# Scores of two heads in two row groups of the TensorE array, in units of two full PSUM banks, maximum unit beside exponential unit

## The reference, cut to what matters

```
qkv = x @ Wqkv + bqkv                      # 16 heads of 16 dimensions
att = softmax(mask(q @ k.T * 16**-0.5))    # causal, 512 x 512 for each head
y   = (att @ v) @ Wout + bout
x1  = layernorm(x + y)
h   = silu(x1 @ w1.T * s1) * (x1 @ w2.T * s2)     # 256 -> 1024
h   = gelu(h @ h1.T * sh1);  h = gelu(h @ h2.T * sh2)   # 1024 -> 1024, twice
out = layernorm(x1 + h @ w3.T * s3)               # 1024 -> 256
```

## Time and profile before

| | |
|---|---|
| median of 2 runs | 2169.16 us (2168.17 to 2170.16) |
| span of the profiled execution | 2166.8 us |
| TensorE, matmuls | 2118.4 us busy (98% of the span) |
| VectorE, ScalarE, GpSimd | 1259.9 (58%), 1316.1 (61%), 492.9 us (23%) |
| chain that ended last | TensorE 89% of it |
| score matmuls in that chain | maxima (line 1116) 7%, exponentials (line 1104) 6% |

### The profile page before, as it was taken

The page is one execution under the profiler, slowest core; times in us unless marked ns, Lnnn a source line. Parts: engine busy times, 40 slices in busy tenths (PEclk is TensorE's granted clock), DMA queues, the critical chain, the costliest instruction groups (busy, mean ns, idle before and its releaser), DMA issues.

```text
span 2166.8 us, 52048 instructions
## 1 busy us (share of the span) xinstructions
PE 2118.4 (98%) x16294; PEld 1878.8 (87%) x16294; DVE 1259.9 (58%) x3928; ACT 1316.1 (61%) x2807; POOL 492.9 (23%) x899
## 2 busy tenths in 40 slices
PE   8789999999999999999999999999999999999998
PEld 4368889989889888899989889988999898988998
DVE  7765555556555565556556565565556556565452
...
PEclk9889999999999999999999999999999999999999
...
GB/s 275 239 120 63 77 71 70 61 81 64 90 65 61 82 74 69 75 69 73 61 81 64 90 64 62 81 76 73 71 76 70 56 82 69 83 64 37 37 6 10
DMA packets 95940, 167.69 MB, mean 77 GB/s; under 512 B 19204, under 2 KB 38404, under 8 KB 95672
## 3 DMA queue, kind: packets, MB, share of 16 engines
...
## 4 chain that ended last, share of the span: by engine, by line
PE 89%; DVE 1%; DMA 0%; issue 0%; SPq 0%; ACT 0%; POOL 0%; POOLq 0%; DVEq 0%
PE ring L1241 44%; PE ring L1226 10%; PE pM L1116 7%; PE pS L1104 6%; PE pO L1164 6%; PE ring L1254 5%; PE ring L1176 4%; PE ring L1206 2%; PE ring L1196 2%; PE ring L1148 1%; PE ring L1215 1%; DMA qk_d<-c 0%; SPq L614 0%; DVE full_g L960 0%; DMA Qs<-nm 0%
## 5 line engine op out<-in xcount | busy, mean ns | idle before, releaser
L921 DVE CUSTOM_DVE_ANT_0 pM<-pM,mask 128x512 f32<-128x512 f32 (+3 forms) x1024 | 498.7, 502 | 366.1 <-PE pM L1116 292.3
L1241 PE MATMUL ring<-Yhi,H 128*128 128x256 f32 x1984 | 501.7, 289 | 0.0
L1241 PE MATMUL ring<-Xhi,H 128*128 128x256 f32 x1984 | 497.9, 288 | 0.0
L1241 PE MATMUL ring<-Ylo,H 128*128 128x256 f32 x1984 | 489.2, 282 | 0.0
L1241 PE MATMUL ring<-Xlo,H 128*128 128x256 f32 x1984 | 486.4, 282 | 0.0
L1241 PEld LDWEIGHTS ring<-Ylo,H 128*128 128x128 f32 x1984 | 377.8, 190 | 7.2 <-issue 3.4
L1241 PEld LDWEIGHTS ring<-Yhi,H 128*128 128x128 f32 x1984 | 377.0, 190 | 7.1 <-issue 3.4
L1241 PEld LDWEIGHTS ring<-Xlo,H 128*128 128x128 f32 x1984 | 379.1, 191 | 0.8
L1241 PEld LDWEIGHTS ring<-Xhi,H 128*128 128x128 f32 x1984 | 378.4, 191 | 1.0 <-issue 0.2
L1116 PE MATMUL pM<-Ks,Qs 128*128 128x512 f32 x992 | 304.2, 340 | 20.6 <-DVE mx L921 9.0
L865 ACT ACTIVATE Yhi<-ring,cols 128x256 fp32r<-128x256 f32 x248 | 117.8, 475 | 266.8 <-PE ring L1241 170.1
...
## 6 DMA issues: line engine op xcount, KB each, us to landing
...
```

Source lines behind the costliest of these rows:

```text
L921: nc.vector.tensor_tensor_reduce(pM[:, h % 2, 0:n], pM[:, h % 2, 0:n], mask[:, T - n:T], 1.0, NEG, ALU.add, ALU.max, mx[:, t, h:h + 1]).th ...
L1241: mm = nc.tensor.matmul(to, w, x_part, start=(k == 0 and m == 0), stop=(k == KB - 1 and m == 1))
```

## The change

- `Qs` and `Qx` lose the dimension that held each head alone: a stack has both heads of a pair in its rows, as `Ks` has. The zeros (two memsets on VectorE, two on GpSimd, semaphores `pads`, `pads_x`) go, and in the head one ScalarE copy takes the place of two.
- A score matmul takes the 50 rows of one head only, at partition 0 or at partition 64: two heads of a pair lie in two row groups of the array, and write to two banks of `pS` or `pM` (bank `s` for head `s`).
- A group has five steps `exp:off:g:e` and five steps `max:off:g:e`. Step e = 0, 1 is 512 columns of pair e; e = 2, 3 is 384 and 128 columns (blocks `kt` 1 and 3, `t` 2 and 0) of a pair; e = 4 is 256 columns of both pairs. So each step fills both banks. TensorE waits for a bank just before its first matmul into it. ScalarE has two instructions of 512 columns in each step, in place of 11 units of 512 or 384 columns; VectorE still has 16 maxima with the same columns.
- `probs_a`, `probs_b` and the new `probs_c` hold the probabilities, `probs_x` and `probs_y` over the feed-forward buffers go, and `Yhi_t` moves from `Ks` to the probabilities. GpSimd has 7 instructions a group in place of 8; the last has 4 x 128 columns and comes after both exponentials of its step.
- In all lists `max:0:g+1:e` stands directly ahead of (in the head also at other places near) `exp:0:g:e`. So all 16 maxima of a group lie in the exponential stage; none is left in the Gelu stages. The rest of the lists keeps its order, but for small shifts. The number of feed-forward matmuls does not change.

```diff
-EXP_UNITS = [0, 4, 8, 10, 11]
+UNITS_G, MASKS = 10, 7
 ORDER = """
-max:0:1:3:0 max:0:1:3:1 y:-1:0:0 table:0:Exp:0 exp:0:0:0 y:-1:0:1 max:0:1:3:2 max:0:1:3:3 exp:0:0:1 y:-1:1:0
-exp:0:0:2 h2:-2:1:0:0 exp:0:0:3 exp:0:0:4 h2:-2:1:0:1 exp:0:0:5 max:0:1:2:0 exp:0:0:6 stack:0:2 y:-1:1:1
...
+y:-1:0:0 table:0:Exp:0 y:-1:0:1 max:0:1:0 exp:0:0:0 y:-1:1:0 h2:-2:1:0:0 max:0:1:1 exp:0:0:1 h2:-2:1:0:1 max:0:1:2
+exp:0:0:2 stack:0:2 y:-1:1:1 max:0:1:3 exp:0:0:3 h2:-2:1:1:0 max:0:1:4 exp:0:0:4 h2:-2:1:1:1 table:0:Gelu:1
...
+h2:-2:1:7:1 h_rest:-2:h2:1:7 x1_turn:-1:0 table:0:Exp:2 ffn_out:-2:1:0 x1_turn:-1:1 max:0:2:0 exp:0:1:0 ffn_out:-2:1:1
+max:0:2:1 exp:0:1:1 gu:-1:0:0 max:0:2:2 exp:0:1:2 gu:-1:0:1 ffn_hi:-1:0:0 gu:-1:0:2 max:0:2:3 exp:0:1:3 ffn_hi:-1:0:1
+gu:-1:0:3 ffn_hi:-1:0:2 gu:-1:0:4 ffn_hi:-1:0:3 gu:-1:0:5 stack:0:3 ffn_hi:-1:0:4 max:0:2:4 exp:0:1:4 gu:-1:0:6
...
+h1:-1:0:7:0 table:0:Exp:4 h_rest:-1:h1:0:7 h1:-1:0:7:1 qk:1:0 max:0:3:0 exp:0:2:0 h2:-1:0:0:0 h2:-1:0:0:1 max:0:3:1
+exp:0:2:1 h2:-1:0:1:0 max:0:3:2 exp:0:2:2 h2:-1:0:1:1 max:0:3:3 exp:0:2:3 h2:-1:0:2:0 h2:-1:0:2:1 max:0:3:4 exp:0:2:4
+table:0:Gelu:5 h_act:-1:h2:0:0 pv:0:2:1 h_rest:-1:h2:0:0 h2:-1:0:3:0 h_rest:-1:h2:0:1 stack:1:0 h2:-1:0:3:1 o_out:0:2
...
+h2:-1:0:7:1 qk:1:1 ffn_out:-1:0:0 table:0:Exp:6 max:1:0:0 exp:0:3:0 stack:1:1 ffn_out:-1:0:1 gu:-1:1:0 gu:-1:1:1
+ffn_hi:-1:1:0 max:1:0:1 exp:0:3:1 gu:-1:1:2 ffn_hi:-1:1:1 gu:-1:1:3 max:1:0:2 exp:0:3:2 ffn_hi:-1:1:2 gu:-1:1:4
+ffn_hi:-1:1:3 max:1:0:3 exp:0:3:3 gu:-1:1:5 ffn_hi:-1:1:4 gu:-1:1:6 ffn_hi:-1:1:5 gu:-1:1:7 max:1:0:4 exp:0:3:4
...
+        def blocks_of(e):
+            if e < 2:
+                return [(0, e, 0)]
+            if e < 4:
+                return [(1, e - 2, 0), (3, e - 2, T - P)]
+            return [(2, p, p * T // 2) for p in range(PAIRS)]
...
+                        g, e = a                       # ScalarE, kind "exp"
+                        for s in range(2):
+                            nth = g * UNITS_G + 2 * e + s
+                            act.wait_ge(e_ready, b * UNITS + nth + 1)
+                            nc.scalar.activation(unit_probs(e)[:, s], pS[:, s], ACT.Exp, scale=SCALE).then_inc(exp_done, 1)
...
+                        need(dve, m_split, 2 * (b * NG + g))     # VectorE, kind "max"
+                        for s in range(2):
+                            nth = b * UNITS + g * UNITS_G + 2 * e + s
+                            dve.wait_ge(m_ready, nth + 1)
+                            held(dve)
+                            for kt, p, at in blocks_of(e):
+                                t, n = TB - 1 - kt, e_cols(kt)
+                                top = nc.vector.tensor_tensor_reduce(
+                                    pM[:, s, at:at + n], pM[:, s, at:at + n], mask[:, T - n:T], 1.0, NEG, ALU.add, ALU.max,
+                                    mx[:, t, 2 * p + s:2 * p + s + 1])
+                            top.then_inc(m_done, 1)
...
+                        nth = b * UNITS + g * UNITS_G + 2 * e    # TensorE, kind "max"; "exp" alike with pS, exp_done, e_ready
+                        blocks = blocks_of(e)
+                        for m, (kt, p, at) in enumerate(blocks):
+                            t, n = TB - 1 - kt, e_cols(kt)
+                            for s in range(2):
+                                rows = slice(SROWS * s, SROWS * s + STACK)
+                                if m == 0:
+                                    need(pe, m_done, nth + s - 1)
+                                mm = nc.tensor.matmul(pM[:, s, at:at + n], Q[rows, p, t * P:(t + 1) * P],
+                                                      K[rows, p, 0:n], start=True, stop=True)
+                                if m == len(blocks) - 1:
+                                    mm.then_inc(m_ready, 1)
```

More of the change, by code:

```diff
@@ L127 @@
-weight_test:0:9 raw:0:10 v:1:3 max:1:1:2:3 exp:1:0:7 max:1:1:1:0 qk:1:2 exp:1:0:8 stack:1:2 y:0:0:0 y:0:0:1
-y:0:1:0 max:1:1:1:1 exp:1:0:9 exp:1:0:10 max:1:1:1:2 y:0:1:1 max:1:1:1:3 max:1:1:0:0 max:1:1:0:1 ln1_stats:0
-max:1:1:0:2 max:1:1:0:3 weights:0:10 pv:1:0:1 neg_split:1:1 weight_test:0:10 neg_max:1:1 ln1:0 low_bits:0 qk:1:3
-exp:1:1:0 exp:1:1:1 x1_turn:0:0 exp:1:1:2 x1_turn:0:1 max:1:2:3:0 exp:1:1:3 exp:1:1:4 o_out:1:0 weight_flag:0
+table:0:Exp:0 qk:0:0 raw:0:0 qk:0:1 stack:0:0 raw:0:1 columns:0 qk:0:2 max:0:0:0 stack:0:1 raw:0:2 max:0:0:1 v:0:0
@@ L131 @@
+max:1:1:0 exp:1:0:0 max:1:1:1 exp:1:0:1 max:1:1:2 exp:1:0:2 den_turn:0 rec_load:0 weight_test:0:9 raw:0:10 v:1:3
+max:1:1:3 exp:1:0:3 qk:1:2 stack:1:2 y:0:0:0 y:0:0:1 y:0:1:0 max:1:1:4 exp:1:0:4 y:0:1:1 ln1_stats:0 weights:0:10
+pv:1:0:1 neg_split:1:1 weight_test:0:10 neg_max:1:1 ln1:0 low_bits:0 qk:1:3 exp:1:1:0 x1_turn:0:0 x1_turn:0:1
+exp:1:1:1 o_out:1:0 weight_flag:0
 """
 FIRST_ORDER = """
-table:0:Exp:0 max:0:2:3:1 table:0:Gelu:1 table:0:Exp:2 max:0:2:3:2 gu:-1:0:0 gu:-1:0:1 exp:0:1:5 max:0:2:3:3
@@ L150 @@
-load_x:0 max:0:3:0:3 h_act:-1:h2:0:6 h2:-1:0:6:1 h_rest:-1:h2:0:5 neg_split:0:3 h2:-1:0:7:0 neg_max:0:3
-h_rest:-1:h2:0:6 h2:-1:0:7:1 h_rest:-1:h2:0:7 h_act:-1:h2:0:7 max:1:0:3:0 qk:1:1 ffn_out:-1:0:0 table:0:Exp:6
-ffn_out:-1:0:1 exp:0:3:0 exp:0:3:1 max:1:0:3:1 gu:-1:1:0 gu:-1:1:1 exp:0:3:2 ffn_hi:-1:1:0 exp:0:3:3 max:1:0:3:2
-max:1:0:3:3 ffn_hi:-1:1:1 gu:-1:1:2 gu:-1:1:3 exp:0:3:4
+table:0:Exp:0 max:0:2:0 table:0:Gelu:1 table:0:Exp:2 gu:-1:0:0 gu:-1:0:1 exp:0:1:2 max:0:2:1 ffn_hi:-1:0:0 gu:-1:0:2
@@ new lines @@
+exp:0:1:3 ffn_hi:-1:0:1 gu:-1:0:3 ffn_hi:-1:0:2 gu:-1:0:4 ffn_hi:-1:0:3 gu:-1:0:5 max:0:2:2 ffn_hi:-1:0:4 gu:-1:0:6
+exp:0:1:4 gu:-1:0:7 load_xT:1 pv:0:1:1 max:0:2:3 ffn_hi:-1:0:5 h1:-1:0:0:0 h1:-1:0:0:1 h_rest:-1:h1:0:0 ffn_hi:-1:0:6
+max:0:2:4 h1:-1:0:1:0 h1:-1:0:1:1 ffn_hi:-1:0:7 table:0:Gelu:3 h_act:-1:h1:0:0 h1:-1:0:2:0 h_rest:-1:h1:0:1
+h1:-1:0:2:1 h1:-1:0:3:0 h_rest:-1:h1:0:2 h_act:-1:h1:0:1 h1:-1:0:3:1 stack:0:3 h_act:-1:h1:0:2 h_rest:-1:h1:0:3
+h1:-1:0:4:0 neg_split:0:2 h_act:-1:h1:0:3 h_rest:-1:h1:0:4 h1:-1:0:4:1 h_act:-1:h1:0:4 h_rest:-1:h1:0:5 h1:-1:0:5:0
@@ new lines @@
+h1:-1:0:5:1 neg_max:0:2 h1:-1:0:6:0 h1:-1:0:6:1 h1:-1:0:7:0 h_act:-1:h1:0:5 h1:-1:0:7:1 h_act:-1:h1:0:6
+h_act:-1:h1:0:7 table:0:Exp:4 h_rest:-1:h1:0:6 h_rest:-1:h1:0:7 h2:-1:0:0:0 exp:0:2:0 max:0:3:0 qk:1:0 max:0:3:1
+exp:0:2:1 h2:-1:0:0:1 exp:0:2:2 h2:-1:0:1:0 exp:0:2:3 max:0:3:2 stack:1:0 o_out:0:1 h2:-1:0:1:1 h2:-1:0:2:0 max:0:3:3
+h_rest:-1:h2:0:0 h_rest:-1:h2:0:1 exp:0:2:4 table:0:Gelu:5 h2:-1:0:2:1 h_act:-1:h2:0:0 max:0:3:4 pv:0:2:1
+h_act:-1:h2:0:1 h_rest:-1:h2:0:2 h2:-1:0:3:0 h2:-1:0:3:1 h_act:-1:h2:0:2 h2:-1:0:4:0 h_act:-1:h2:0:3 h2:-1:0:4:1
@@ L581, in move @@
                         Q, K = stacks(steps, off, g)
-                        first = steps is HEAD and off == 0
-                        if first and g < PICKED:
+                        if steps is HEAD and off == 0:
                             continue
@@ L1097, in iteration @@
                             pe.wait_ge(nm_done, b * NG + g + 1)
-                        if steps is HEAD and off == 0 and g == 0 and u == 0:
+                        if steps is HEAD and off == 0 and g == 0 and e == 0:
                             pe.wait_ge(head_in, PICKED * HEAD_COPIES)
-                        need(pe, exp_done, b * UNITS + nth - 1)
-                        for p in sorted({p for p, _ in heads}):
-                            wide = [k for k, (m, _) in enumerate(heads) if m == p]
-                            first, last = heads[wide[0]][1], heads[wide[-1]][1]
-                            mm = nc.tensor.matmul(pS[:, nth % 2, n * wide[0]:n * (wide[-1] + 1)],
-                                                  K[:, p, kt * P:(kt + 1) * P],
-                                                  Q[:, p, first:last + 1, kt * P:T], start=True, stop=True)
```

327 lines of the change are left out of this document (119 added, 208 removed).

## The result

The changed kernel takes **2262.53 us** (2 runs, 2261.11 to 2263.96) against 2169.16: a ratio of 1.0436 with a 95% interval of 1.0406 to 1.0467. It is slower, and 60 us above the forecast of 2202; just beyond the upper end of the range.

A forecast was written before the change was run, and what follows sets the result against it. TensorE was taken to bound the steady part: -8.8 (pairs) + 5.8 (switches) + 5.4 (waits), rounded +2.3 us a batch, over 14.5 batches +33 us on 2169.2, so 2202 us (+1.5%); 8-in-10 range 2120 to 2260 us.

The forecast's parts named there:

- TensorE bounds the kernel: Steady part: TensorE is busy 648.7 of 649.5 us, so each us saved there comes out unless it waits.
- The saving and the switches, -8.8 and +5.8: TensorE's scores: pairs at once save 8.8 us a batch; switching tiling costs 0.30 us a visit, 5.8 a batch.
- the sum: Per batch: -8.8 saving, +5.8 switches, +5.4 waits, +2.3 us rounded; scores before taken as 4.69 us a group.
- The page's rule that I set aside: TensorE weight loads overlap a running matmul only if row groups differ; set aside because whole-array 512-column scores start 0.24 us apart.
- the rival of exposed weights: First pair of each unit and 128-column pairs: weight loads exposed behind each switch, 0.5 us a visit, 2239 us; 18%.
- What the banks cost, +5.4 a batch: Exponential stages: TensorE waits for VectorE to free both `pM` banks, and at group 2's end; 5.4 us a batch.
- my walk: Unit-by-unit estimate of TensorE's waits in the four groups' exponential stages, 5.4 us a batch in sum.
- The head, taken as 0: Head: about 1 us gained, 1 to 4 us possibly lost to coupled banks; taken as 0.
- The Gelu stages, taken as unaffected: Gelu stages lose only maxima; an `h1` or `h2` block is 1.92 us of TensorE against 0.8 of ScalarE, nothing late.
- the serial pairs: Score pairs run one after the other: +8.8 us a batch, 2297 us; chance 10%.

The follow-up runs named there:

- the short-maxima run: The changed kernel with VectorE's maxima cut to the last 128 columns of each block, row pairs kept: 2185.9 us, 130.7 a batch.
- run 8: The changed kernel with whole-array scores in the head and first steady stretch only, row pairs in the rest: 2254.2 us.
- run 1: The changed kernel with every score matmul reading both heads' rows, so whole array and pairs in turn: 2261.2 us, 136.3 a batch.
- run 4: The kernel before with its one-head score matmuls cut to that head's 50 rows, order and banks untouched: 2428.7 us, ratio 1.1203.
- run 9: The changed kernel with whole-array scores and maximum units 2 to 4 of each group moved into the Gelu stages: 2307.9 us.
- run 13: The changed kernel, row pairs kept, with maximum units 3 and 4 moved into the Gelu stages and their VectorE maxima listed by bank: 2225.8 us.

## Why the prediction was wrong, step by step

- **TensorE bounds the kernel:** right, and the reason why every wait that came in shows in full.
- **The saving and the switches, -8.8 and +5.8:** the switch was right: 0.09 in, 0.09 out and 0.10 on the second matmul behind, 0.28 us for the forecast's 0.30. Not in the sum was what a pair pays behind another pair in the same rows: 0.10 us in a unit of 512 columns (0.334 for 0.235) and in one of 256, 0.16 in one of 384 and 128. Where nothing waits, a visit costs 0.86 us (512 or 256 columns) or 0.91 us (384 and 128) over the plain distances around it; the forecast had 0.77 to 0.78. That is 17.4 us a batch for the 15.8 of the sum. But the scores of the kernel before also cost more than the 18.8 that the sum took for them: behind a maximum of 128 columns the next matmul holds TensorE for 0.17 us instead of 0.12.

```profile
1139.46 0.34 PE L1241 MATMUL ring<-Xhi,H 128*128 128x256 f32 x1
1139.63 0.28 PE L1241 MATMUL ring<-Xlo,H 128*128 128x256 f32 x1
```

  By the starts of all scores they cost 19.6. So the pairs saved about 2.2 us a batch, not 3.0.
- **The page's rule that I set aside:** the Trainium skill (TensorE: Matmul & The Clock Gate, What overlaps and what doesn't) ties the overlap of a weight load with a running matmul to differing row groups. The trace does not bear that out as it stands, for the whole array or for row pairs: the second pair's weights are loaded at 932.35, while the first pair, in the same rows, runs from 932.24. But that load starts 0.11 us behind the first pair, where on the whole array the load for the score at 1052.71 starts with the one ahead of it, at 1052.47, and the second pair comes 0.10 us later. So the rival of exposed weights had the right place: it asked for 0.20 us more a visit, it needed 0.05, and the visits show 0.11 (0.08 to 0.14).
- **What the banks cost, +5.4 a batch: this is the step that failed.** It measured about 7.0. Added up from start-to-start distances over ten batches, the waits before maxima are 2.0, 1.4, 1.2 and 1.8 us in groups 0 to 3, 6.4 in all, where the kernel before has 0.6 and my walk had 1.5, 1.1, 0.35 and 1.35. The places that the walk named were right, and it did ask for the second bank of a unit, which comes free a maximum after the first (0.65 us at unit 1 of group 2, 0.76 at unit 4 of group 0 and unit 3 of group 3). Two things in it were not. In group 2 it left out the step of the projection (`qk`, L874) that stands in VectorE's list just ahead of the maxima, and had 0.25 us at unit 1 where 0.69 were lost:

```profile
999.28 0.75 DVE L874 SCALAR_TENSOR_TENSOR c<-ring,cols,c 128x512 fp32r<-128x512 f32 x1 [1.66 <-ACT c L738]
999.95 0.69 DVE L857 CUSTOM_DVE_ANT_0 pM<-pM,mask 128x512 f32<-128x512 f32 x1
```

  And it let VectorE be through with a unit of 384 and 128 columns too soon. A bank is handed over with its last matmul. In unit 2 of group 0 that matmul ends 0.5 us behind the unit's first start (937.48 for 936.98), VectorE starts 0.2 us behind its end, where the walk had 0.04, and then takes 1.49 us instead of 1.4. The second head of unit 3 starts at 939.39, 2.4 us behind the first matmul of unit 2:

```profile
937.70 0.57 DVE L857 CUSTOM_DVE_ANT_0 pM<-pM,mask 128x384 f32<-128x384 f32 x1 [0.69 <-PE pM L1060]
```

  At unit 3 the walk had 0.2 and 0.1 us in groups 0 and 2, and some 0.7 and 0.5 came. The end of group 2's stage was nearly right: 0.52 us for the select and 0.65 for ScalarE against 1.0.
- **The clock, in no term:** 31 us at 1.2 GHz in the steady part, some 1.2 us a batch by the batches without it. Of that, 0.8 is what the matmuls outside scores and `pv` lose over the short-maxima run, and the rest lies in the waits above. Before, it never fell between 147 us and the last 3, so the trace of before gave no reason to expect it.
- **The head, taken as 0:** 15.5 us, half of it with the pairs and their lower clock (run 8), the other half with either form.
- **The Gelu stages, taken as unaffected:** right.

By size: forecast +33; the thirteen batches gave 3.5 us each more than forecast (+45), the head 15 and the tail 4, less the 3 us that the forecast had for the other batch and a half. Of the 3.5 us the banks are 1.6, the smaller saving 0.8 and the clock outside the waits 0.8; some 0.3 have no place. No rival's time came true: those of the serial pairs (2297) and of exposed weights (2239) lie on both sides of it. Both put the loss in TensorE's own work, and with VectorE's maxima cut short the kernel stood at 2186. What the forecast lacked was a rival in which its own wait term was too small.

Left open: the 3.3 us a batch that stay with whole-array scores and short maxima are, by the same distances, 1.1 at the end of group 2's stage, 1.4 of waits for VectorE still (2.0 against 0.6), and 0.8 of scores (20.5 us against 19.6 in the kernel before, most of it in the units of 384 and 128 columns); no run takes these apart. Why the second pair's load starts late is not shown either. And what brings the clock down is seen in which runs have it, not shown by one that changes the clock alone: run 1 has most of the changed kernel's waits before maxima (4.9 us a batch for 6.4) without pairs, and no stretch, and run 4 has row tiles without waits and none. But run 9, on the whole array with one wait of 2.2 us a batch, has it too (0.99), so long waits do it without pairs, and run 13, with pairs and one wait of 1.2 us a batch, has none.
